# Layer 2 linear attention: two VectorE steps exchanged with their neighbours, and layer 3 experts in 39 blocks

## The reference, cut to what matters

```python
q, k, v = (hidden @ W for W in (Wq, Wk, Wv))          # per head 64, 64, 128
s = clip(hidden @ Ws, -32, 32)                        # per head 64 slots
z = cumlogsumexp(s); p = exp(s - z); g = exp(z_before - z)
...
hk = hk * g_t[:, :, None, :] + k_t[..., None] * p_t[:, :, None, :]   # per token
ok = einsum('bhk,bhkm->bhm', q_t, hk)
pv = softmax(ok)
hv = hv * g_t[..., None] + p_t[..., None] * v_t[:, :, None, :]
ov = einsum('bhm,bhmv->bhv', pv_t, hv)
...
o = o * rsqrt(mean(square(o)) + EPS) * g_norm_weight
out = (o * (g * sigmoid(g))) @ Wo                     # g = hidden @ Wg
```

```python
top_logits, top_idx = top_k(x @ gate_w, 2);  top_w = softmax(top_logits)
for e in range(8):
    h = silu(x @ w0[e]) * (x @ w1[e])
    out = out + cw[:, e:e + 1] * (h @ wo[e])
```

## Time and profile before

| | |
|---|---|
| median of 3 runs | 2171.97 us (2171.43 to 2173.82) |
| profiled execution, its own time | 2193.66 us |
| its span, first to last instruction | 2192.1 us |
| mean granted TensorE clock | 0.92 |
| TensorE, VectorE, ScalarE, GpSimd busy | 86%, 64%, 31%, 26% of the span |

### The profile page before, as it was taken

The page is one execution under the profiler, slowest core; times in us unless marked ns, Lnnn a source line. Parts: engine busy times, 40 slices in busy tenths (PEclk is TensorE's granted clock), DMA queues, the critical chain, the costliest instruction groups (busy, mean ns, idle before and its releaser), DMA issues. The chain is left out here.

```text
span 2192.1 us, 35525 instructions
## 1 busy us (share of the span) xinstructions
PE 1875.1 (86%) x13312; PEld 1444.0 (66%) x13312; DVE 1399.3 (64%) x3037; ACT 680.2 (31%) x1205; POOL 565.3 (26%) x552
## 2 busy tenths in 40 slices
PE   5943479971999999999999997989988988989995
PEld 2341357760888888888888886455566876756663
DVE  4476355548777777777777776476656777533334
ACT  2231334441333232323333332235534323222221
POOL 0234615550021212212121211532332103401111
PEclk9975579995999999999999998999998996999998
DMA  9329224426000000000000100000001006111114
GB/s 325 122 74 296 80 82 152 151 97 199 1 1 22 1 23 12 12 23 1 23 1 23 32 1 1 1 1 2 2 1 51 27 1 240 69 37 47 47 47 134
DMA packets 100639, 134.97 MB, mean 62 GB/s; under 512 B 11616, under 2 KB 73980, under 8 KB 99968
## 3 DMA queue, kind: packets, MB, share of 16 engines
q1 hardware_dynamic: 89344, 102.16, 14.7%
q0 software_dynamic: 11136, 30.62, 3.9%
HBM read 81.94 MB, written 50.81 MB: 61 GB/s over the span
## 5 line engine op out<-in xcount | busy, mean ns | idle before, releaser
L1114 POOL TENSOR_TENSOR a_rstd<-a_ms,consts 128x8 f32<-128x8 f32 x32 | 52.4, 1638 | 590.0 <-DVE a_ms L1466 590.0
L110 PE MATMUL a_ring<-a_w_hi,l_xnT_hi 128*128 128x256 f32 x512 | 157.3, 307 | 0.0
L110 PE MATMUL a_ring<-a_w_hi,l_xnT_lo 128*128 128x256 f32 x512 | 144.2, 282 | 0.0
L110 PE MATMUL a_ring<-a_w_lo,l_xnT_hi 128*128 128x256 f32 x512 | 144.0, 281 | 0.0
L2456 POOL DMA_INDIRECT l_slots_in<-xn,f_row_of x96 | 98.5, 1026 | 97.6 <-DVE f_row_of L2750 36.6
L2983 POOL DMA_INDIRECT l_pairs_out<-f_yb,f_to_row x96 | 96.2, 1002 | 101.6 <-ACT f_yb L2958 64.2
L1219 PE MATMUL a_pab<-a_w_o,a_oT 128*128 128x256 f32 x512 | 119.2, 387 | 1.2 <-ACT a_oT L1358 1.2
L1421 DVE RECIPROCAL a_rT<-a_rT 128x256 f32<-128x256 f32 x64 | 111.4, 1742 | 0.0
L1219 PEld LDWEIGHTS a_pab<-a_w_o,a_oT 128*128 128x128 f32 x512 | 100.2, 201 | 11.6 <-ACT a_oT L1358 1.6
L1704 PE MATMUL b_ring<-b_keys,b_qm 32*128 32x128 f32 (+2 forms) x896 | 91.2, 339 | 14.9 <-DVE b_nm L1917 9.4
L1465 DVE TENSOR_REDUCE a_ms<-a_on 128x8 f32<-128x1024 f32 x32 | 39.0, 1220 | 100.9 <-ACT a_on L1378 100.9
(11 more groups left out here) (495 smaller groups left out, 5069.6 us busy)
## 6 DMA issues: line engine op xcount, KB each, us to landing
l_slots_in<-l_zeros SPq DMA_DIRECT2D x4, 3120.0 KB, 22.3
f_xb<-l_slots_in SPq DMA_DIRECT2D x11, 1040.0 KB
f_gate_up_w<-l_pairs_out SPq DMA_DIRECT2D x16, 512.0 KB, 8.7
l_slots_in<-l_zeros SPq DMA_DIRECT2D x4, 1300.0 KB, 15.4
f_xb<-l_slots_in SPq DMA_DIRECT2D x40, 130.0 KB, 2.0
f_down_w<-L_ffn_w_down_dram SPq DMA_DIRECT2D x1, 4096.0 KB
f_gate_w<-L_ffn_w_dram SPq DMA_DIRECT2D x2, 2048.0 KB, 11.1
f_up_w<-L_ffn_w_dram SPq DMA_DIRECT2D x2, 2048.0 KB, 19.8
```

The source lines that it names most:

```text
L110: ins = pe.matmul(out, a, b, start=start and k == 0, stop=stop and k == 2, **kw)
L1114: pool.tensor_tensor(rstd[:], ms[:], core.consts[:, C_HALF:C_HALF + 8], ALU.pow).then_inc(s["rstd_ready"], 1)
```

## The change

In `unit` of VectorE's program `prefix_k(u)` now stands directly behind `prefix_v(u)`, ahead of `project_s`; and the second half of the reciprocal, `project_r(n, kn, 1)`, stands ahead of `emit(u - 1, ...)`. The layer 3 experts get one block fewer: with 4,096 pairs in blocks of 128 and 8 experts, at most 32 + 7 blocks are ever needed. 39 is odd, so the slots of layer 3 are cleared one row a piece, by three transfers of 13 blocks each. Layer 1 keeps its blocks and its clearing. The wait for the last stores counts those of each ring slot.

```diff
                 prefix_v(u)
+                prefix_k(u)
                 if not last:
                     project_s(n, kn)
-                prefix_k(u)
                 if not first:
                     gated(u - 1)
...
                 dve.tensor_tensor(heads8(wt[:]), heads8(ex[:]), den[:].unsqueeze(2).to_broadcast([P, 8, DK]),
                                   ALU.mult).then_inc(s["wt_ready"], 1)
+                if not last:
+                    project_r(n, kn, 1)
                 if not first:
                     emit(u - 1, (k - 1) % PER)
-                if not last:
-                    project_r(n, kn, 1)
                 dve.wait_ge(s["w_turned"], u + 1)
...
-        self.blocks = self.K * TILES + self.E
+        self.blocks = self.K * TILES + self.E - self.FEWER
...
-        self.CLEARS = 4
-
     def clear(self, sp, zeros):
-        n = self.blocks // (2 * self.CLEARS)
-        for k in range(self.CLEARS):
-            to = self.xs[k * n * 2 * P:(k + 1) * n * 2 * P, :].rearrange("(n q i) d -> q n (i d)", q=P, i=2)
-            sp.dma_start(to, zeros[:].unsqueeze(1).to_broadcast([P, n, 2 * ROW])).then_inc(self.cleared, 16)
+        for rows, zero in self.clearings(zeros):
+            sp.dma_start(rows, zero).then_inc(self.cleared, 16)
...
 class Slots3(Slots):
+    FEWER, CLEARS = 1, 3
+
+    def clearings(self, zeros):
+        n = self.blocks // self.CLEARS
+        for k in range(self.CLEARS):
+            yield (self.xs[k * n * P:(k + 1) * n * P, :].rearrange("(n q) d -> q n d", q=P),
+                   zeros[:, 0:ROW].unsqueeze(1).to_broadcast([P, n, ROW]))
+
...
             for k in range(RING):
-                sp.wait_ge(stored[k], 16 * (NB // RING))
+                sp.wait_ge(stored[k], 16 * len(range(k, NB, RING)))
```

More of the change, by code:

```diff
@@ L2478 @@
 class Slots1(Slots):
+    FEWER, CLEARS = 0, 4
+    def clearings(self, zeros):
+        n = self.blocks // (2 * self.CLEARS)
+        for k in range(self.CLEARS):
+            yield (self.xs[k * n * 2 * P:(k + 1) * n * 2 * P, :].rearrange("(n q i) d -> q n (i d)", q=P, i=2),
+                   zeros[:].unsqueeze(1).to_broadcast([P, n, 2 * ROW]))
     def place(self, st):
```

## The result

The changed kernel takes 2140.9 us (median of 4 runs, 2137.64 to 2144.51), the kernel before beside it 2171.81 us (2171.43 to 2173.82). The ratio is 0.9856 with a 95% interval of [0.9835, 0.9877]: 30.9 us faster, where 33.4 us were forecast (2138.5 us, range 2134 to 2150). Four executions is few, and they spread over 7 us; the interval is worth 26.7 to 35.8 us, so the time alone can't tell 31 from 33 us. The traces can.

The account below looks back on a forecast made before the run. TensorE was taken to bound both changed stages. 30 units x 0.92 = 27.6 us in the linear attention plus 5.8 us for one block made 33.4 us, so 2171.97 - 33.4 = 2138.5 us, range 2134 to 2150.

Parts of the forecast that it names:

- TensorE bounds both stages: Layer 2 linear attention and layer 3 experts: TensorE busy 97.5 of 100 us and 60 of 60 us.
- Gap 1: Linear attention, `ok` waiting for the k-sums after the last `q` matmul: closes, worth 0.53 us a unit.
- Gap 2: Linear attention, `weights` waiting for `wT` after the last `g1` matmul: closes, worth 0.39 us a unit.
- Rival (a): Linear attention: gain only 0.62 us a unit, 18.6 us over 30 units, so 2147.5 us in all; chance 0.13.
- VectorE becomes the bound (b): Linear attention: covers of 0.08 to 0.14 us used up; chain 0.1 to 0.3 us too long, 2141.5 to 2147.5 us; chance 0.14.
- `gated` starts as before: VectorE in linear attention: multiplication for `gated` still starts at 1037.36, the same instructions standing ahead of it.
- The late clipping costs nothing: Linear attention: clipping moves back 1.5 us behind the k-sums; ScalarE's exponential keeps 1.0 us of cover before the scan.
- Slower rival (d): Linear attention: later clipping holds up exponential, scan, `lgT`, `wT` and TensorE; 2.2 us lateness would eat 33.4 us; chance 0.03.
- One block, 5.8 us: Layer 3 experts: blocks pass TensorE at a fixed pace of 5.82 us, so one fewer gains 5.8 us.
- The clearing, zero: Layer 3 slots, cleared during layer 0: three transfers with 4,992 pieces stay hidden even at twice the time; cost zero.
- Sum: Whole kernel: 27.6 us from linear attention plus 5.8 us from layer 3, 33.4 us in all.
- The 21.7 us between profiled execution and median: Whole kernel: profiled execution 2193.66 us against median 2171.97; place unknown, difference carried over as it is.

Follow-up runs that it names:

- the reciprocal behind the masks: Changed kernel with the second half of the reciprocal moved on behind the masking of am: 2154.73 us beside 2161.31 for the changed kernel on the same chip.
- the k-sums alone: Kernel before with one edit, the k-sums put ahead of the clipping: 2155.75 us, ratio 0.9923.
- the part alone: Changed kernel with both linear attention edits undone, leaving 39 blocks and one-row clearing: 2165.5 us, ratio 0.9967 to the kernel before.
- the same kernel with 40 blocks: One-row clearing by four transfers of 10 blocks, 40 blocks and VectorE's order as in the kernel before: 2172.44 us, ratio 0.9996.
- that of the second chip: The changed kernel run again, unaltered, on another chip: 2161.31 us, ratio 0.9843 to the kernel before.
- the four from the first chip: Kernel before with only k-sums moved, 2155.75 us; only reciprocal moved, 2163.74; only 39 blocks and one-row clearing, 2165.5; one-row clearing with 40 blocks, 2172.44.
- the four from the second chip: Changed kernel unaltered, 2161.31 us; with reciprocal behind am's masking, 2154.73; turning of k ahead of weights, 2169.06; clipping behind gated and k's copy, 2185.93.

## Why the prediction was right, point by point

- *TensorE bounds both stages, so an edit is worth the TensorE gap that it closes*: right. With its gaps closed TensorE is busy 100 of 100 us, and 1.7 us less on VectorE's way to `wT` changes nothing (the reciprocal behind the masks).
- *Gap 1, 0.53 us a unit*: right, 0.55 us alone. That the lead isn't lost ahead of `weights` follows from the residual's 0.97 us of idle time; the k-sums alone show it.
- *Gap 2, 0.39 us a unit*: the mis-sized term. It measured 0.30 us. The step that failed is that `weights` could follow `g1` at the pace of the 256-column matmuls, 0.12 us; it follows at 0.21 us, however early `wT` is. Unlike gap 1, for which unit 0 showed the same pair without a wait, I had no row of this pair without one. That unit 0 has neither gap is true of `ok` alone: `weights` there starts 0.40 us behind `g1` (578.35 to 578.75), as late as `wT` lets it.
- *Rival (a), only the idle column comes back (0.62 us a unit)*: falls, with 0.85 us measured. It was short by 0.23, my start-to-start count long by 0.07.
- *VectorE becomes the bound (b)*: doesn't happen, though it is near. TensorE shows no wait that returns each unit. But my step that `gated` starts as before, since the same instructions stand ahead of it, was wrong by 0.12 us (2.26 in place of 2.14), and that was about all the cover there was: the one ahead of turning the logits is 0.05 us and not 0.13, and `turn_out`, for which I had 0.09 us, starts 1.05 us behind the products before it (1022.64 to 1023.69) where it is 1.03 us in before (1038.31 to 1039.34). That the covers held was in part luck.
- *The late clipping costs nothing*: right, the scan shows no wait in the kernel after. *Slower rival (d)*: its mechanism is real where the clipping is put later still, and dearer than I had it: beyond the scan's cover (1.1 us in the kernel after, 1023.04 to 1024.15, where I had 1.0) it costs nearly in full.
- *One block, 5.8 us*: right, 5.8 us between the traces of before and after and 5.2 in that of the part alone, 5.6 against the same kernel with 40 blocks. *The clearing, zero*: right.
- *Sum*: 30 x 0.85 + 5.8 = 31.3 us against 30.9 measured; the forecast's 33.4 is high by the 30 x 0.09 of gap 2, less the 30 x 0.02 that gap 1 gave more than counted. The time alone would not have told: its 26.7 to 35.8 us shut out (a) with 24.4, but hold 31.3, 33.4 and (b) at 0.1 us a unit. The periods did.
- *The 21.7 us between profiled execution and median, carried over unexplained*: they lay for the most part in layer 1, ahead of the linear attention, and touched no term.

## What to carry to other kernels

Price a gap on TensorE from start to start against the same pair of instructions somewhere without a wait (a first unit is good for that); the idle column gave 0.62, the bare matmul pace 0.92, and 0.85 was right. Where two edits stand on one loop, run each alone: that the parts added up to the whole is what told a slow transition on TensorE from a VectorE short of time. And when an operation is moved back, look at which engine reads it: the clipping could go behind six small operations for nothing and behind two more for 22 us.

## What the runs showed of the hardware that I had not expected

One stretch that no edit here changes takes 67.7 to 94.9 us from trace to trace, and most of what sets profiled executions apart lies in it. It runs from SyncE's first load of the down biases for layer 1's experts to its first load of a block for them, and two things run side by side in it: layer 1's attention and GpSimd's scattering of the token rows into slots. Its busy time in the kernel after, in the execution of the result and then in that of the second chip:

```profile
206.00:273.80 67.80, 26.93 (x446) 17.76 (x446) 27.59 (x61) 25.52 (x50) 48.27 (x47) 0.70 0.41 143
```
```profile
206.00:299.50 93.50, 39.78 (x468) 25.81 (x467) 29.18 (x62) 28.51 (x57) 46.34 (x46) 0.55 0.30 102
```

VectorE, ScalarE and GpSimd have the same work in both within 3 us, and TensorE is busy 13 us longer, at a granted clock of 0.55 in place of 0.70. But the stretch doesn't end by the same work in both. In the first the attention's last operation ends at 245.8 us and GpSimd scatters until 268.3; up to 244.6 us the granted clock is 0.84 on the mean, and only in the 29.2 us behind, in which TensorE does nothing, 0.50. In the second the attention itself goes on to 299.0 us. It is 53 us longer there, and the waits (total us, times, longest) say how, first in the execution of the result, then in the other:

```profile
ACT a_sums L897 <- PE a_out L849: 10.2, 12, 2.5
...
DVE a_e L924 <- ACT a_e L891: 6.0, 10, 1.3
```
```profile
DVE a_e L924 <- ACT a_e L891: 46.4, 13, 15.1
ACT a_sums L897 <- remote: 37.1, 7, 14.6
```

No wait of the attention within these windows is longer than 2.5 us in the first; in the second TensorE, VectorE and ScalarE stand still together several times, for 5 to 15 us each. The same splits the ten traces. In the five without such standstills (the kernel after and the four from the first chip) ScalarE's last operation of the attention starts at 240.9 to 243.4 us; in the kernel before and the four from the second chip it starts at 276.9 to 298.1. What holds the engines up, and whether the low clock comes of the waiting, is open.

And the change from `g1` to `weights` on TensorE costs 0.09 us more than the pace of the projections; a reordering only moved it, since it comes with the step to products on 64 rows.
